# Dividing the moves of turned squares between SyncE's and GpSimd's queues in a graph-attention stage

## The reference

```
y = layernorm(x) * (1 + scale(cond)) + bias(cond)
q, k, v = y wq + bq, y wk + bk, y wv + bv          # 4 heads of width 128, q scaled by 128 ** -0.5
scores  = q[src] . k[dst]                          # over 41,250 edges
attn    = exp(scores - max over src) / sum over src
x       = x + (segment_sum(attn * v[dst], src)) wo + bo
y       = layernorm(x) * (1 + scale(cond)) + bias(cond)
x       = x + relu(y m_w1 + m_b1) m_w2 + m_b2
```

## Time and profile before

| | |
|---|---|
| median of 3 runs | 2701.36 us (2696.13 to 2714.99) |
| the profiled execution's own time | 2705.17 us |
| its span, first to last instruction | 2703.4 us |
| mean granted TensorE clock, share of full speed | 0.974 |
| TensorE matmul busy | 2461.2 us (91%) |
| VectorE busy | 1383.2 us (51%) |
| ScalarE busy | 945.6 us (35%) |
| GpSimd busy | 400.1 us (15%) |

### The profile page before, as it was taken

The page is one execution under the profiler, slowest core; times in us unless marked ns, Lnnn a source line. Parts: engine busy times, 40 slices in busy tenths (PEclk is TensorE's granted clock), DMA queues, the critical chain, the costliest instruction groups (busy, mean ns, idle before and its releaser), DMA issues. The chain is left out here.

```text
span 2703.4 us, 27071 instructions
## 1 busy us (share of the span) xinstructions
PE 2461.2 (91%) x9136; PEld 1373.3 (51%) x9136; DVE 1383.2 (51%) x2907; ACT 945.6 (35%) x1615; POOL 400.1 (15%) x405
## 2 busy tenths in 40 slices
PE   8999899998888999788999888999978898998994
PEld 4665545454555554555455455555455554533341
DVE  7986742415664533666551566453265644523343
ACT  5875532114552121554111355212055512201221
POOL 2014120101000200100200100020010012524551
PEclk9999999999999999999999999999999999999997
DMA  6301011313554010555210255401055521559636
GB/s 177 113 21 48 1 42 58 100 51 76 123 127 118 25 36 4 125 129 126 66 54 0 65 127 132 121 25 35 4 122 128 125 63 56 190 194 317 218 90 207
DMA packets 145973, 259.56 MB, mean 96 GB/s; under 512 B 52521, under 2 KB 53001, under 8 KB 143495
## 3 DMA queue, kind: packets, MB, share of 16 engines
q1 hardware_dynamic: 122310, 211.13, 28.7%
q0 software_dynamic: 20784, 41.80, 4.8%
q10 hardware_dynamic: 2741, 4.89, 0.6%
HBM read 207.68 MB, written 27.34 MB: 87 GB/s over the span
## 5 line engine op out<-in xcount | busy, mean ns | idle before, releaser
L1804 PE MATMUL psum<-cols,rows 128*128 128x256 f32 (+1 forms) x1600 | 396.4, 398 | 134.1 <-DMA cols<-w 134.1
L1804 PEld LDWEIGHTS psum<-cols,rows 128*128 128x128 f32 (+1 forms) x1600 | 311.1, 198 | 201.0 <-DMA cols<-w 159.0
L1979 ACT ACTIVATE g_prob<-g_prob,g_row_max 125x1250 f32<-125x1250 f32 x160 | 214.1, 1338 | 519.8 <-DVE g_row_max L1912 519.8
L1724 PE MATMUL psum<-cols,w 128*128 128x500 f32 (+1 forms) x1120 | 393.2, 510 | 1.2 <-PEq L94 1.2
L1790 PE MATMUL psum<-g_k_cols,g_q_cols 128*125 128x512 f32 (+1 forms) x960 | 362.9, 515 | 4.1 <-DVE g_row_max L1909 4.1
L1909 DVE CUSTOM_DVE_ANT_0 g_prob<-psum,ln_count 125x1250 f32<-125x1250 f32 x160 | 233.6, 1460 | 237.9 <-PE psum L1790 237.9
L1724 PEld LDWEIGHTS psum<-cols,w 128*128 128x128 f32 x1120 | 209.8, 189 | 173.2 <-issue 165.1
L1790 PEld LDWEIGHTS psum<-g_k_cols,g_q_cols 128*125 128x125 f32 x960 | 180.9, 189 | 175.9 <-issue 161.9
L1921 DVE STREAM_TRANSPOSE w<-g_prob 128x1280 f32<-128x1280 f32 x160 | 241.0, 1506 | 33.4 <-DMA cols<-w 27.5
L1985 ACT ACTIVATE g_prob<-g_prob,g_row_max 125x1250 f32<-125x1250 f32 x160 | 214.0, 1338 | 101.1 <-DVE g_row_max L1899 101.1
L2563 PE MATMUL psum<-m_ew,m_x_cols 128*64 128x256 f32 (+1 forms) x576 | 152.5, 495 | 6.9 <-DMA cols<-in_L_ffn_expert_w,m_weights_of 6.3
(11 more groups left out here) (344 smaller groups left out, 3343.1 us busy)
## 6 DMA issues: line engine op xcount, KB each, us to landing
cols<-w SPq DMA_DIRECT2D x1280, 80.0 KB
m_eb<-in_L_ffn_expert_b SPq DMA_DIRECT2D x54, 192.0 KB, 6.0
w<-in_L_gnn_m_w SPq DMA_DIRECT2D x8, 1024.0 KB
slot_rows<-p_kf SPq DMA_DIRECT2D x1, 7128.0 KB, 32.8
rows<-slot_rows SPq DMA_DIRECT2D x54, 132.0 KB, 3.4
m_ew<-in_L_ffn_expert_w SPq DMA_DIRECT2D x4, 1536.0 KB, 11.3
w<-in_L_mix_W SPq DMA_DIRECT2D x4, 1024.0 KB, 5.4
w<-in_L_gnn_wq SPq DMA_DIRECT2D x4, 1024.0 KB, 5.1
```

What stands on the lines that cost most here:

```text
L1724: ins = c.pe.matmul(c.bank(group_bank(g), width), wt[:, k, o * 128:(o + 1) * 128], y_cols[:, k, start:start + width], start=(k == 0), stop ...
L1804: ins = pe.matmul(c.bank(6 + g % 2, 256).rearrange("p (u a i) -> p u a i", u=2, a=SIDE), rows[0:r, j, h * 128:(h + 1) * 128], turned_keys[ ...
L1979: s.activation(prob[0:P, u, 0:N], prob[0:P, u, 0:N], ACT.Exp, bias=row_max[:, u, 1:2], accum_out=row_max[:, u, 2:3]).then_inc(exp_made, 1)
```

## The change

- In the gnn, `turn_sp` becomes `move_squares(eng, l, g, moves, done)`, which both queues call. SyncE issues ten of the sixteen moves of each pair, GpSimd six: the four with equal quarters, and (0, 1) and (2, 3). Each queue has its own pair of semaphores, and everyone who waited for sixteen moves waits for both (`wait_turned`): TensorE before part 0 of `weigh`, VectorE before it transposes into a used slot, SyncE after the loop.
- GpSimd's ten additions of `bo` no longer run together before the loop: one stands behind its moves of each of the first ten pairs. SyncE's wait for them, and its load of `m_b2`, move from before pair 10 to before pair 13.
- In the performer's query loop ScalarE copies the transposed features one step earlier (those of step n - 1 before the exponentials of step n), and VectorE divides one step later (step n - 3 behind the maximum of step n).
- Elsewhere semaphores are merged (`x_stat` and `x_mean` into `x_step`, `h_stat` and `h_mean` into `h_step`, `prm_out` and `shared_prm_in` into `prm_passed`, `g_clipped` and `u_clipped` into `e_clipped`), with the counts adjusted; no instruction there is added, removed or moved.

```diff
-KEPT_SEMS = 8
+KEPT_SEMS = 10
@@ attention_dve
             for n in range(Q_STEPS):
                 highest(n)
-                if n >= 2:
-                    divide(n - 2)
+                if n >= 3:
+                    divide(n - 3)
+            divide(Q_STEPS - 3)
             project_dve(0)
@@ attention_act
-            for n in range(Q_STEPS + 2):
-                if n >= 2:
-                    if n >= 4:
-                        s.wait_ge(out_mm, n - 3)
+            for n in range(Q_STEPS + 1):
+                if n >= 1:
+                    if n >= 3:
+                        s.wait_ge(out_mm, n - 2)
                     for e in range(2):
-                        s.wait_ge(qf_turned, 2 * n - 3 + e)
-                        s.copy(qf_cols[:, n % 2, e], qf_turned_out(e)).then_inc(qf_cols_made, 1)
+                        s.wait_ge(qf_turned, 2 * n - 1 + e)
+                        s.copy(qf_cols[:, (n - 1) % 2, e], qf_turned_out(e)).then_inc(qf_cols_made, 1)
@@ gnn
+    MOVES = [(of, to) for of in range(SIDE) for to in range(SIDE)]
+    POOL_MOVES = [(of, of) for of in range(SIDE)] + [(0, 1), (2, 3)]
+    SP_MOVES = [move for move in MOVES if move not in POOL_MOVES]
@@
-        def turn_sp(l, g):
-
-            sp = c.sp
+        def move_squares(eng, l, g, moves, done):
+
             s, pair = g % 2, PAIRS * l + g
-            sp.wait_ge(squared, 2 * pair + 2)
+            eng.wait_ge(squared, 2 * pair + 2)
             if g >= 2:
-                sp.wait_ge(weighed, pair - 1)
-            for of in range(SIDE):
-                for to in range(SIDE):
-                    load(sp, turned[s][quarter(to), of], square[s][quarter(of), to]).then_inc(turned_in[s], 16)
+                eng.wait_ge(weighed, pair - 1)
+            for of, to in moves:
+                load(eng, turned[s][quarter(to), of], square[s][quarter(of), to]).then_inc(done[s], 16)
+
+        def wait_turned(eng, s, count):
+
+            eng.wait_ge(turned_in[s], 16 * len(SP_MOVES) * count)
+            eng.wait_ge(turned_in_pool[s], 16 * len(POOL_MOVES) * count)
@@ layer_sp
             for g in range(PAIRS):
-                if g == PAIRS // 2:
+                if g == NT + 3:
                     sp.wait_ge(bo_added, NT * (l + 1))
                     load_bias_row("m_b2", l)
-                turn_sp(l, g)
+                move_squares(sp, l, g, SP_MOVES, turned_in)
             for s in range(TURNED_SLOTS):
-                sp.wait_ge(turned_in[s], 16 * SIDE * SIDE * PAIRS // 2 * (l + 1))
+                wait_turned(sp, s, PAIRS // 2 * (l + 1))
@@ weigh (layer_pe)
-                    pe.wait_ge(turned_in[g % 2], 16 * SIDE * SIDE * ((PAIRS * l + g) // 2 + 1))
+                    wait_turned(pe, g % 2, (PAIRS * l + g) // 2 + 1)
@@ turn_squares (layer_dve)
                 if n % 2 == 0 and pair >= 2:
-                    v.wait_ge(turned_in[s], 16 * SIDE * SIDE * (pair // 2))
+                    wait_turned(v, s, pair // 2)
@@ layer_pool
             g.wait_ge(bias_rows_in, 16 * (3 * l + 2))
-            for t in range(NT):
-                g.tensor_tensor(x[:, t, :], x[:, t, :], bias_rows[0:P], ALU.add).then_inc(bo_added, 1)
+            g.wait_ge(v_mm, NT * (l + 1))
+            for pair in range(PAIRS):
+                move_squares(g, l, pair, POOL_MOVES, turned_in_pool)
+                if pair < NT:
+                    g.tensor_tensor(x[:, pair, :], x[:, pair, :], bias_rows[0:P], ALU.add).then_inc(bo_added, 1)
...
```

More of the change, by code:

```diff
@@ L83, in __init__ @@
         (self.edges_gathered, self.gnn_x_in, self.gnn_wq_in, self.gnn_q_mm, self.sum_out, self.odd_sum_out,
-         self.slots_blank, self.shared_w1_in) = (ctx.enter_context(nc.semaphore(name, num=FIRST_SEM + n)) for n, name in enumerate(
-             ("edges_gathered", "gnn_x_in", "gnn_wq_in", "gnn_q_mm", "sum_out", "odd_sum_out", "slots_blank", "shared_w1_in")))
+         self.slots_blank, self.shared_w1_in, *self.gnn_turned_in_pool) = (ctx.enter_context(nc.semaphore(name, num=FIRST_SEM + n)) for n, name in enumerate(
+             ("edges_gathered", "gnn_x_in", "gnn_wq_in", "gnn_q_mm", "sum_out", "odd_sum_out", "slots_blank", "shared_w1_in",
+              "gnn_turned0_in_pool", "gnn_turned1_in_pool")))
         self.ident = ctx.enter_context(nc.sbuf_tensor("ident", [128, 128], F32))
@@ L205, in performer @@
     hidden_made, cond_mm, cond_made = c.sems("hidden_made", "cond_mm", "cond_made")
-    x_stat, x_mean, x_var, x_std, x_rstd, x_low, x_ratio, x_normed = c.sems(
-        "x_stat", "x_mean", "x_var", "x_std", "x_rstd", "x_low", "x_ratio", "x_normed")
-    h_stat, h_mean, h_var, h_std, h_rstd, normed = c.sems("h_stat", "h_mean", "h_var", "h_std", "h_rstd", "p_normed")
+    x_step, x_var, x_std, x_rstd, x_low, x_ratio, x_normed = c.sems(
+        "x_step", "x_var", "x_std", "x_rstd", "x_low", "x_ratio", "x_normed")
+    h_step, h_var, h_std, h_rstd, normed = c.sems("h_step", "h_var", "h_std", "h_rstd", "p_normed")
     h_turned, h_cols = c.sems("p_h_turned", "p_h_cols")
@@ L674, in x_stats_dve @@
             v.wait_ge(x_in[t], 32)
-            v.bn_stats(x_stats[:, t, :], x[:, t, :]).then_inc(x_stat, 1)
-            v.wait_ge(x_stat, t + 1)
-            v.bn_aggr(x_mv[:, t, :], x_stats[:, t, :]).then_inc(x_mean, 1)
+            v.bn_stats(x_stats[:, t, :], x[:, t, :]).then_inc(x_step, 1)
+            v.wait_ge(x_step, 2 * t + 1)
+            v.bn_aggr(x_mv[:, t, :], x_stats[:, t, :]).then_inc(x_step, 1)
         def x_vars_dve(b):
@@ L684, in x_vars_dve @@
             lo, hi = X_BATCHES[b]
-            v.wait_ge(x_mean, hi)
+            v.wait_ge(x_step, 2 * hi)
             v.tensor_scalar(x_r[:, 0, lo:hi], x_mv[:, lo:hi, 1], EPS, None, ALU.add).then_inc(x_var, 1)
@@ L724, in h_stats_dve @@
             v = c.dve
[L725 to L728, removed]
+            v.bn_stats(stat[:, t, :], x[:, t, :]).then_inc(h_step, 1)
+            v.wait_ge(h_step, 2 * t + 1)
+            v.bn_aggr(mv[:, t, :], stat[:, t, :]).then_inc(h_step, 1)
+            v.wait_ge(h_step, 2 * t + 2)
             v.tensor_scalar(rstd[:, t:t + 1], mv[:, t, 1:2], EPS, None, ALU.add).then_inc(h_var, 1)
@@ L1508, in gnn @@
     turned_in = c.sems("g_turned0_in", "g_turned1_in")
+    turned_in_pool = c.gnn_turned_in_pool
     weighed, out_made = c.sems("g_weighed", "g_out_made")
@@ L2064, in moe @@
     back_dram = nc.dram_tensor("slot_outputs", [2 * N + S * HALF, D], F32)
-    prm_in, gate_in, b2_in, w2_in, b1_in, prm_out, shared_prm_in = c.sems(
-        "r_prm_in", "r_gate_in", "r_b2_in", "r_w2_in", "r_b1_in", "r_prm_out", "r_shared_prm_in")
+    prm_in, gate_in, b2_in, w2_in, b1_in, prm_passed = c.sems("r_prm_in", "r_gate_in", "r_b2_in", "r_w2_in", "r_b1_in",
+                                                              "r_prm_passed")
     consts_made, prm_step, raw_made, prm_made = c.sems("r_consts_made", "r_prm_step", "r_raw_made", "r_prm_made")
@@ L2084, in moe @@
     stored = [c.sem(f"e_stored{u}") for u in range(U)]
-    place_made, slot_turned, x_made, up_mm, e_biased, g_clipped, u_clipped = c.sems(
-        "e_place_made", "e_slot_turned", "e_x_made", "e_up_mm", "e_biased", "e_g_clipped", "e_u_clipped")
+    place_made, slot_turned, x_made, up_mm, e_biased, e_clipped = c.sems(
+        "e_place_made", "e_slot_turned", "e_x_made", "e_up_mm", "e_biased", "e_clipped")
     e_sig_made, e_glu_step, glu_made, turned, t_made = c.sems("e_sig_made", "e_glu_step", "e_glu_made", "e_turned",
@@ L2190, in route_sp @@
             sp.wait_ge(prm_made, 2)
-            load(sp, param_dram[:, :], prm[:]).then_inc(prm_out, 16)
-            sp.wait_ge(prm_out, 16)
-            load(sp, shared_prm[:], param_dram[EXPERTS, :].partition_broadcast(128)).then_inc(shared_prm_in, 16)
+            load(sp, param_dram[:, :], prm[:]).then_inc(prm_passed, 16)
+            sp.wait_ge(prm_passed, 16)
+            load(sp, shared_prm[:], param_dram[EXPERTS, :].partition_broadcast(128)).then_inc(prm_passed, 16)
         def route_pool():
@@ L2430, in shared_act @@
             s = c.act
-            s.wait_ge(shared_prm_in, 16)
+            s.wait_ge(prm_passed, 32)
             s.wait_ge(b1_in, 32)
@@ L2446, in shared_dve @@
             q = shared_prm
-            v.wait_ge(shared_prm_in, 16)
+            v.wait_ge(prm_passed, 32)
             for n, (start, width, k) in enumerate(GROUPS):
@@ L2612, in glu_dve @@
             g_, u_ = h[u][:, 0:FFN_I], h[u][:, FFN_I:2 * FFN_I]
-            v.tensor_scalar(g_, g_, q[:, 3:4], q[:, 5:6], ALU.min, ALU.max).then_inc(g_clipped, 1)
-            v.tensor_scalar(u_, u_, q[:, 4:5], q[:, 6:7], ALU.min, ALU.max).then_inc(u_clipped, 1)
+            v.tensor_scalar(g_, g_, q[:, 3:4], q[:, 5:6], ALU.min, ALU.max).then_inc(e_clipped, 1)
+            v.tensor_scalar(u_, u_, q[:, 4:5], q[:, 6:7], ALU.min, ALU.max).then_inc(e_clipped, 1)
             v.wait_ge(e_sig_made, i + 1)
@@ L2617, in glu_dve @@
             v.wait_ge(e_glu_step, i + 1)
-            v.wait_ge(u_clipped, i + 1)
```

(3 more changed lines are left out.)

## The result

The changed kernel took 2545.56 us (median of 4 runs, 2538.86 to 2550.87) against 2700.0 for the one before (a fourth run has joined the three of the table above); the ratio is 0.942, interval 0.937 to 0.946. The direction was right and so was the queue that was named as the bound; the size was not.

What follows compares the result with a forecast made beforehand. SyncE's DMA queue, not the transfers or VectorE, was taken to bound the attention loops. Terms -104.6 + 13 + 4 - 9.5 - 6 - 8.6 = -112 took 2705.2 to 2593, the median 3.8 lower: 2589 us; 80% range 2563 to 2655.

Steps and rivals of the forecast that it cites:

- the second waits: Attention loops: an additional semaphore wait for TensorE (80 times) and VectorE (72), taken as 0, 8 us at most.
- the query loop: Performer's query loop: TensorE's eight waits of 1.07 us for ScalarE's copy go and the gain is passed on, -8.6 us.
- TensorE's own work is 8.79 us a pair: Attention loops: pair distance of 10.13 us less the 1.34 of wait shown, taken as TensorE's pace without waits.
- rival 3: Attention loops: GpSimd's direct DMA is as cheap as SyncE's, so TensorE alone bounds them; 2567 us, chance 17%.
- GpSimd's price: GpSimd's queue in the attention loops: spacing of its direct DMA moves, taken as 1.30 us each from indirect DMAs.
- waits inside the loops: Attention loops: TensorE's waits of 104.6 us go, less 13 for GpSimd's first ten pairs and 4 for long issues.
- first waits: Start of each attention loop: TensorE's wait falls from 7.38 to 5.0 us, -9.5 us over four loops.
- busy time: Attention loops: with the long waits gone, all run near 177.2 us busy at the better granted clock, -6 us.
- rival 2: GpSimd's queue: direct DMA simply dear, 2653 us at spacing 1.50, about 2890 at 1.96; slower end 6%, 1.4 to 1.6 10%.
- Rival 1: Attention loops: VectorE's two transpositions of 1.50 us a pair block GpSimd's moves, +117 us, 2810 in all; chance 6%.
- Rival 4: Attention loops: moves land later or second waits cost; two us more landing gives 2650, three 2690; chance 6%.
- Rival 5: Division of moves between the queues: the split is not what it says; ruled out by counting, no chance given.

Runs made afterwards that it cites:

- pool2: The changed kernel with GpSimd issuing two of the sixteen moves of a pair and SyncE fourteen, instead of six and ten: 2608.64 us.
- dve_ports: The changed kernel plus unread VectorE work behind every second transposition, two float32 SBUF copies in even pairs, one addition in odd: 2543.29 us.

## Why the prediction was right or wrong

**What was right.** SyncE's issuing was the bound; the wait for moves goes; the additions cost nothing between the moves; the second waits leave no idle time in the trace; the query loop gives 8.6 (8.1 and 7.9 measured) and passes it on. That TensorE would be the next bound was right for the last ten pairs of a loop; for the first ten the sum had GpSimd.

**The step that failed** is "TensorE's own work is 8.79 us a pair". It was worked out as the distance of two pairs less the idle time shown between them. But a row of matmuls that has to wait loses the overlap with the one ahead and runs its first matmul longer; the trace books that as busy time. Without a wait a pair takes 8.52 (`pool2` and the changed kernel show both numbers side by side). The same step stood under rival 3, whose 2567 set the low end of the range, so the range could not hold the result whatever GpSimd's price was: with the restarts alone taken off, 2567 becomes 2551, and 2563 was its end.

In the loops the terms went as follows.

| Term | forecast | measured |
|---|---|---|
| waits inside the loops | -104.6 + 13 + 4 | -104.6 |
| first waits | -9.5 | 29.5 to 15.6: -13.9 |
| busy time | -6 | 714.9 to 686.3: -28.6 |
| sum | -103 | -147 |

The busy time divides by the table above: 16.2 us are the restarts, which the sum did not have, and (43.0 - 18.3) / 2 = 12.4 are the clock. The forecast had 6 for the clock, since it took the loops at 0.98 as undisturbed; they too were at 0.50 behind their first wait of 7.4 us and once more inside, and with 3.9 us of wait less of that is left.

**GpSimd's price** was the second error, and as large in the sum: 1.30 from the nearest indirect rows, 0.50 measured, under even the 0.63 that was to bound it from below. The gap of 0.30 behind each indirect DMA is not there behind the direct ones. What else made the indirect ones dearer was not tested. The number of rows may be part of it: six of the ten gathers of 80 rows take 0.91 us and four 1.06 to 1.17, the scatters of 125 rows 1.19 (median), and a straight line from 0.91 through 1.19 gives about 0.6 at 32 rows, an estimate. The price cost the forecast 13 + 4 us of waits and 4.4 of first waits. That puts the forecast at 2589 - 21 = 2568 with the right price, and at 2545 with the right busy time, where the measurement is. Rival 3 was the case that came, at 17%. One sum of rival 2 was off, without weight here: at a spacing of 1.50 the mean pair is 9.9, so 27 us less and not 33, and its 2653 should be 2659.

**The other rivals.** Rival 1, blocking by VectorE: excluded for transpositions and score reads by moves of 0.50 beside them. The trap that the Trainium skill describes (SBUF — State Buffer, the box on DVE blocking DMA and the section "A bandwidth-pool intuition that's wrong (but worth ruling out)") is real here for float32 copies between SBUF tensors: the page has GpSimd's DMA blocked until VectorE's operation ends plus some 115 ns, and the trace of `dve_ports` agrees with 0.09 to 0.10 us in 40 of 40 pairs. Its example of a DMA of 620 ns stretched to some 3100 shows in no run here, where the longest is 0.80. The attention loop has no such copy, so the kernel pays nothing. Rival 2, a dear direct DMA: excluded. Rival 4, landing later: GpSimd's moves land in 2.7 us (median), the value that was taken from the scatters, and at the start of a loop TensorE goes 2.1 us behind SyncE's last issue, as before; the round trip that it rests on is real, sets the pace at thirteen moves on one queue, and at twelve in the pairs with a long issue. Rival 5 could be ruled out from the code.

**What stays open.** What the pauses in GpSimd's queue are in which it waits for nothing shown. The changed kernel has three of 2.9 us, behind which TensorE waits 0.1 us at most; with fifteen moves it does wait. With two, four and eight moves single idle times of 4 to 10 us are marked in the same way, most of them 2.9 us longer than the usual wait for squares in their place. Then SyncE's single long issues, 13 of over 0.9 us in the changed kernel, and the reason for the restart's 0.27 us. The profiled execution's span is 166 us shorter, where the medians differ by 154, and the loops and the query loop are 156 of it. Of the other 10 us, 8 lie behind the last loop. That part lasts 525.3 us before, 517.5 in the changed kernel, 522.4 in its repetition and 518.6 to 524.6 in the other runs, though no instruction there was added, removed or moved, so it differs by that much from one execution to the next.

## What to carry to other kernels

A queue that only issues DMAs can be the bound of a loop while no engine and no transfer is: count its issues by its spacing. When a wait goes away, more goes than the idle time shown, by the restart behind each wait and by the clock that falls behind the long ones; take the pace of the freed engine from a stretch without waits, such as within a pair, and let the optimistic end of the range hold it. When work is divided between queues, check the round trip (last input to landing, and back) and not only each queue's rate, and leave room in it for the queue's longest issues. When blocking between engines is looked for, read single instructions and where they end, not the mean of a group.

## What the runs showed of the hardware

A direct DMA of 32 partitions x 2560 bytes costs GpSimd's queue 0.50 us (496 to 581 ns, 480 of them) and SyncE's 0.63, with single issues of up to 1.7 us in the changed kernel (2.3 before); GpSimd's indirect ones cost 0.91 to 1.66 and a gap of 0.30. GpSimd's direct DMAs run at the same pace beside VectorE's transpositions, PSUM reads and float32 additions. A float32 copy between SBUF tensors on VectorE (0.69 us) holds one that starts with it or in it until 0.09 to 0.10 us behind its end (0.61 to 0.80 us instead of 0.50, in 40 of 40 pairs). A wait of TensorE between rows of matmuls costs 0.27 us more than the idle time in the trace. Behind an idle time of 3.9 us or 7.4 us its granted clock was 0.50, and a row of ten matmuls took 3.9 to 4.6 us instead of 2.32.
